# Two attention layers with experts on one core: projections moved among the first scores and beside the routing, score tiles issued around the transposed pair

## What is computed

```
x = x + tanh(g_xattn[0]) * attention0(layernorm(x), ctx)     # 16 heads of 16
x = x + tanh(g_ffn[0])   * experts(layernorm(x))             # 8 experts, top 2, weights 256x256
x = x + tanh(g_xattn[1]) * attention1(layernorm(x), ctx)
x = x + tanh(g_ffn[1])   * bitlinear_ffn(layernorm(x))       # 256 -> 1024 -> gelu -> 256, activations to 8 bit, weights ternary

attention: q = x Wq^T + bq, k = ctx Wk^T + bk, v = ctx Wv^T + bv
           softmax(q k^T / 4) v, heads joined, times Wo^T, plus bo
```

## Time and profile before

| | us |
|---|---|
| time, median of 3 runs (lowest, highest) | 765.19 (763.31, 765.99) |
| the profiled execution, its time | 762.36 |
| the profiled execution, its span | 760.5 |
| PE busy | 690.9 (91%) |
| DVE busy | 534.3 (70%) |
| ACT busy | 432.4 (57%) |
| POOL busy | 164.2 (22%) |
| mean granted TensorE clock | 0.973 |

### The profile page before, as it was taken

The page is one execution under the profiler, slowest core; times in us unless marked ns, Lnnn a source line. Parts: engine busy times, 40 slices in busy tenths (PEclk is TensorE's granted clock), DMA queues, the critical chain, the costliest instruction groups (busy, mean ns, idle before and its releaser), DMA issues.

```text
span 760.5 us, 10162 instructions
## 1 busy us (share of the span) xinstructions
PE 690.9 (91%) x3595; PEld 331.7 (44%) x3600; DVE 534.3 (70%) x1140; ACT 432.4 (57%) x568; POOL 164.2 (22%) x300
## 2 busy tenths in 40 slices
PE   4899999899999999998999989998999899987887
PEld 2433333354544445444554445443444344332444
DVE  2577886578886687868787688865686749775334
ACT  2227666763346633665336733476776677758735
POOL 7105244630010310121101410114210301021132
PEclk9769999999999999999999999999999999999999
DMA  7749578521211501224211411126023212200000
GB/s 242 205 126 335 181 226 266 169 55 32 42 43 29 167 11 34 61 80 98 44 36 37 125 44 43 43 71 199 11 64 91 77 50 57 58 2 1 22 8 28
DMA packets 39026, 66.74 MB, mean 88 GB/s; under 512 B 5184, under 2 KB 13888, under 8 KB 38720
## 3 DMA queue, kind: packets, MB, share of 16 engines
q1 hardware_dynamic: 38128, 65.57, 30.0%
q10 hardware_dynamic: 848, 0.53, 0.2%
HBM read 38.29 MB, written 27.26 MB: 86 GB/s over the span
## 4 chain that ended last, share of the span: by engine, by line
PE 59%; DVE 14%; ACT 10%; issue 8%; POOL 8%; POOLq 0%; DVEq 0%; ACTq 0%
PE psO L799 11%; PE psS L771 8%; PE psX L724 6%; PE psT L785 6%; DVE mx L1194 6%; PE psX L860 5%; PE psX L836 4%; PE psX L861 4%; PE psX L862 4%; ACT pt L1017 3%; PE psX L744 3%; POOL parts L588 2%; DVE xs L1325 2%; ACT qf L962 2%; ACT parts L963 1%
## 5 line engine op out<-in xcount | busy, mean ns | idle before, releaser
L1017 ACT ACTIVATE pt<-psT 128x1024 f32<-128x1024 f32 x256 | 261.7, 1022 | 220.6 <-PE psT L785 218.1
L1194 DVE TENSOR_REDUCE mx<-psS 128x1 f32<-128x512 f32 x512 | 325.7, 681 | 80.5 <-PE psS L771 79.1
L771 PE MATMUL psS<-ks,qs 48*128 48x512 f32 x512 | 152.5, 514 | 15.2 <-DVE mx L1194 13.8
L799 PE MATMUL psO<-pt,vg 128*32 128x512 f32 x1024 | 139.5, 618 | 0.1
L785 PE MATMUL psT<-qs,ks 50*128 50x512 f32 x512 | 118.8, 428 | 6.9 <-ACT pt L1017 5.8
L771 PEld LDWEIGHTS psS<-ks,qs 48*128 48x128 f32 x512 | 59.9, 189 | 130.0 <-issue 73.1
L1325 DVE SCALAR_TENSOR_TENSOR xs<-psX,coef,xs 128x256 f32<-128x256 f32 x128 | 61.9, 483 | 32.4 <-PE psX L862 29.2
L588 POOL TENSOR_TENSOR parts<-qf,parts 128x512 fp32r<-128x512 f32 x30 | 38.3, 1278 | 147.2 <-ACT parts L963 147.2
L785 PEld LDWEIGHTS psT<-qs,ks 50*128 50x128 f32 x512 | 52.6, 189 | 22.4 <-ACT pt L1017 19.5
L860 PE MATMUL psX<-moeh,xh 128*128 128x512 f32 x128 | 57.4, 449 | 4.4 <-DVE xs L1325 4.4
L861 PE MATMUL psX<-moel,xh 128*128 128x512 f32 x128 | 50.7, 396 | 0.0
(11 more groups left out here) (129 smaller groups left out, 765.3 us busy)
## 6 DMA issues: line engine op xcount, KB each, us to landing
ks<-kd SPq DMA_DIRECT2D x64, 192.0 KB, 3.5
qs<-qd SPq DMA_DIRECT2D x64, 192.0 KB, 4.3
kd<-parts SPq DMA_DIRECT2D x16, 512.0 KB, 3.2
qd<-parts SPq DMA_DIRECT2D x16, 512.0 KB, 2.7
kd<-parts SPq DMA_DIRECT2D x16, 256.0 KB, 4.1
qd<-parts SPq DMA_DIRECT2D x16, 256.0 KB, 3.4
ctxb<-in_ctxT SPq DMA_DIRECT2D x7, 512.0 KB, 4.7
xs<-in_x SPq DMA_DIRECT2D x4, 512.0 KB, 6.1
```

The costliest lines, as they stand in the source:

```text
L771: mm(psS[:, i % 3, :], qs[at:at + KR, 2 * g + a, k * P:(k + 1) * P], ks[at:at + KR, 2 * g + a, :], start=True, stop=True).then_inc(pe_s, 1)
L799: i = mm(psO[32 * j:32 * j + 32, :], vg[:, p % 2, k, g * GH + j, :], pt[:, s % RING, j, :], start=k == 0, stop=k == NT - 1, tile_position= ...
L1017: a(pt[:, G % RING, 2 * half:2 * half + 2, :], psT[:], ACT.Exp, scale=SCALE).then_inc(a_exp, 1)
L1194: v.tensor_reduce(mx[:, w // GH % 2, r, col:col + 1], psS[:, i % 3, :], AX.X, ALU.max).then_inc(v_max, 1)
```

## The change

1. Slot order: S of (w, half) is issued as two separate items; one score tile (upper rows), then both transposed tiles with the lower rows first, then the other score tile (lower rows), then PV and the slot's pieces. `s_pair` becomes `s_tile`, and the maxima on DVE follow one by one.
2. The four SPLITs of stage 1 (K and Q) leave slots 0, 2, 4 and 6 of stage 0. K 0 goes ahead of the lead, K 1 to slot -10, Q 0 to slot -7, Q 1 to slot -4; the second XT of sequence 1 moves to slot -12.
3. The two K SPLITs of stage 3 move from slots 0 and 2 of stage 1 to slots 16 and 18.
4. In stages 1 to 4 the VV pieces move from slots 11 and 15 to 6 and 10. In stages 2 to 4 the second layer norm, its XT and its two Q SPLITs move from slots 3 to 10 to slots 13 to 18, beside the routing. (The layer norm's two coefficient sets are then used in swapped order: the `swap` argument.)
5. In stages 5 to 7 both XB stand at slot 15 instead of one at 14 and one at 15.
6. XQ and HQ have four small DVE steps instead of five, and POOL waits for three of them.
7. For the very first and the very last layer norm the small steps run on DVE (LNE, LND), with only the power on POOL; in the tail they stand in another order, and BUSY shrinks from 29 + 4 + 4 + 9 to 20 + 4 + 4.

```diff
     lead = -1
+    put(lead, 20, ("XT", (1,)))
     put(lead, 21, ("RELOAD", (0, 2)))
-    put(lead, 22, ("RELOAD", (0, 3)))
+    put(lead, 22, ("RELOAD", (0, 3)), ("SPLIT", ("K", 1, 1)))
+    put(lead, 25, ("SPLIT", ("Q", 1, 0)))
+    put(lead, 28, ("SPLIT", ("Q", 1, 1)))
...
-    put(0, 0, ("SPLIT", ("Q", 1, 0)), ("LD", ("x3",)))
+    put(0, 0, ("LD", ("x3",)))
     put(0, 1, ("LD", ("w1",)))
-    put(0, 2, ("SPLIT", ("K", 1, 0)))
     put(0, 3, ("LNC", (2, 0, NT)), ("LD", ("w2",)))
-    put(0, 4, ("SPLIT", ("Q", 1, 1)), ("LD", ("k1",)))
-    put(0, 5, ("LNN", (2, 0, 2)))
-    put(0, 6, ("SPLIT", ("K", 1, 1)), ("LNN", (2, 2, 4)))
+    put(0, 4, ("LD", ("k1",)))
+    put(0, 5, ("LNN", (0, 2, 0, 2)))
+    put(0, 6, ("LNN", (0, 2, 2, 4)))
...
-    pair(1, 0, "SPLIT", "K", 3, step=2)
+    pair(1, 16, "SPLIT", "K", 3, step=2)
...
-                put(p, 11, ("VV", (p + 1, 0)))
-                put(p, 15, ("VV", (p + 1, 1)))
+                put(p, 6, ("VV", (p + 1, 0)))
+                put(p, 10, ("VV", (p + 1, 1)))
...
+        two = 2 <= p <= B
         if 2 <= p <= B + 1:
             st(p, 1, p - 2, NT - 1)
             put(p, 1, ("LNC", (p - 2, 0, NT)))
-            put(p, 3, ("LNN", (p - 2, 0, 2)))
-            put(p, 4, ("LNN", (p - 2, 2, 4)))
+            put(p, 20, ("BIAS", (p - 2, 1)))
+        if p == B + 1:
+            put(p, 3, ("LNN", (0, p - 2, 0, 2)))
+            put(p, 4, ("LNN", (0, p - 2, 2, 4)))
             pair(p, 5, "XT")
             pair(p, 9, "SPLIT", "Q", B + p - 2)
-            put(p, 20, ("BIAS", (p - 2, 1)))
...
+            if two:
+                put(p, 13, ("LNN", (1, p - 2, 0, 2)))
+                put(p, 14, ("LNN", (1, p - 2, 2, 4)))
+                pair(p, 15, "XT", step=0)
+                pair(p, 16, "SPLIT", "Q", B + p - 2, step=2)
...
-            put(p, 14, ("XB", (0, 1, 0, NT)))
-            put(p, 15, ("XB", (1, 2, 0, NT)))
+            put(p, 15, ("XB", (0, 1, 0, NT)), ("XB", (1, 2, 0, NT)))
...
-    put(NP, 4, ("OP", (1, b, 0)), ("ST", (b, 0)), ("ST", (b, 1)), ("LNC", (b, 0, 2)), ("LNN", (b, 0, 2)))
-    put(NP, 4, ("OP", (1, b, 1)), ("ST", (b, 2)), ("ST", (b, 3)), ("LNC", (b, 2, 4)))
-    put(NP, 4, ("BUSY", (29,)))
-    put(NP, 5, ("XQ", (0, 2)), ("LNN", (b, 2, 4)), ("XB", (0, NC, 0, 2)), ("BUSY", (4,)), ("XQ", (2, 4)))
-    put(NP, 5, ("F1", (0,)), ("XB", (0, NC, 2, 4)), ("BUSY", (4,)), ("F1", (1,)), ("F1", (2,)), ("F1", (3,)),
-        ("BUSY", (9,)))
+    put(NP, 4, ("OP", (1, b, 0)), ("ST", (b, 0)), ("ST", (b, 1)), ("LNE", (b, 0, 2)), ("OP", (1, b, 1)))
+    put(NP, 4, ("LND", (b, 0, 2)), ("LNN", (0, b, 0, 2)), ("ST", (b, 2)), ("ST", (b, 3)))
+    put(NP, 4, ("LNE", (b, 2, 4)), ("LND", (b, 2, 4)))
+    put(NP, 4, ("BUSY", (20,)))
+    put(NP, 5, ("XQ", (0, 2)), ("LNN", (0, b, 2, 4)), ("XB", (0, NC, 0, 2)), ("BUSY", (4,)), ("F1", (0,)))
+    put(NP, 5, ("XQ", (2, 4)), ("XB", (0, NC, 2, 4)), ("BUSY", (4,)), ("F1", (1,)), ("F1", (2,)), ("F1", (3,)))
...
-    out = [("ST", (0, t)) for t in range(NT)] + [("LNC", (0, 0, NT)), ("SPLIT", ("K", 0, 0)), ("LNV", ())]
+    out = [("ST", (0, t)) for t in range(NT)] + [("LNE", (0, 0, NT)), ("LND", (0, 0, NT)), ("SPLIT", ("K", 0, 0)), ("LNV", ())]
...
-    out += [("VV", (0, 0)), ("VV", (0, 1)), ("LNN", (1, 0, NT))] + [("XT", (c,)) for c in range(NC)]
+    out += [("VV", (0, 0)), ("VV", (0, 1)), ("LNN", (0, 1, 0, NT))]
+    out += [("SPLIT", ("K", 1, 0)), ("XT", (0,))]
...
         if 0 <= w < NP * H:
-            out.append(("S", (w, half)))
+            out.append(("S", (w, half, 0)))
         if 0 <= G < NP * H:
             out.append(("T", (G, half)))
+        if 0 <= w < NP * H:
+            out.append(("S", (w, half, 1)))
...
-                for r in range(2):
+                for r in (1, 0):
                     at = HALF * r
                     i = mm(psT[:, r, :], ks[at:at + KR + MP, 2 * g + half, k * P:(k + 1) * P],
...
+            def variances(b, t0, t1):
+                ...
+                v.tensor_scalar(lnw[:, i, 5, t0:t1], mv[:, i, t0:t1, 1], LN_EPS, None, ALU.add).then_inc(v_ln, 1)
...
+            def coefficients(b, t0, t1):
+                ...
+                v.tensor_tensor(t, r0, r0, ALU.mult).then_inc(v_ln, 1)
...
+                v.tensor_tensor(t, t, ve, ALU.mult).then_inc(v_ln, 1)
...
+                v.tensor_scalar(t, t, -0.5, 1.5, ALU.mult, ALU.add).then_inc(v_ln, 1)
...
+                v.tensor_tensor(r1, r0, t, ALU.mult).then_inc(v_ln, 1)
...
+                v.scalar_tensor_tensor(out=nb, in0=mean, scalar=-1.0, in1=r1, op0=ALU.mult, op1=ALU.mult
+                                       ).then_inc(v_ln, 1)
...
-                v.tensor_scalar(big, big, Q_EPS, None, ALU.max).then_inc(v_hq, 1)
+                v.tensor_scalar(big, big, Q_EPS, 1.0 / 127.0, ALU.max, ALU.mult).then_inc(v_hq, 1)
                 if due(v_hq, i + 2):
                     dve.wait_ge(v_hq, i + 2)
+                v.reciprocal(inv, big).then_inc(v_hq, 1)
                 v.tensor_scalar(deq, big, dqf[:, 1:2], None, ALU.mult).then_inc(v_hq, 1)
-                v.reciprocal(inv, big).then_inc(v_hq, 1)
-                if due(v_hq, i + 4):
-                    dve.wait_ge(v_hq, i + 4)
-                v.tensor_scalar(inv, inv, 127.0, None, ALU.mult).then_inc(v_hq, 1)
```

131 lines of the change are left out of this document (81 added, 50 removed).

## The result

The changed kernel takes 775.47 us (median of 4 executions, 774.1 to 782.5) against 765.53 (763.31 to 765.99); the ratio is 1.0171, 95% interval [1.0138, 1.0205]. Forecast were 745 and faster. The profiled execution took 776.58, its span is 774.8 against 760.5.

A forecast was written before the change was run, and what follows sets the result against it. PE was taken as the bound, with time won only where it waits or runs at 1.2 GHz. Terms 0 - 7.5 - 3 - 4.5 - 3.5 + 0 - 1.5 = -20 us took 765.2 to 745, range 734 to 758.

The forecast's parts named there:

- Start and lead: Up to the first exponential: earlier first S (-2.5 us) offsets the projections and XT added to the lead (+2.8); sum 0.
- so I take the other two at full clock, 0.5 us each with the turn: Lead: only the first of three SPLITs meets the low clock; the other two starve DVE 0.5 us each.
- the sign of success: First exponential at 46 to 50 us would show the forecast right.
- Stage 0: Slots 0 to 8 without their four SPLITs take 17 us instead of 24.5, a gain of 7.5.
- Rival 3: Clock: lead stays at 1.2 GHz, stage 0's slots 0 to 2 and the tail's F1 slow; 753 us, chance 0.10.
- Stage 1: Moving two K SPLITs to slots 16 and 18, and a VV to slot 6, gains 3 us.
- won from the clock: Stage 1: about 1.5 us gained because the clock, at 0.98 there, would be fuller.
- Stages 2 to 4: Moved XT and SPLITs fill the 1.43 us routing wait; -1.5 us a stage, -4.5 in all.
- XB, XQ, HQ: Stages 5 to 7: XB at slot 15 fills PE's wait for POOL, with fewer steps; -1, -2 and -0.5 us.
- The slot order: T freed from a waiting second S gains 8 us; lone second S tiles behind T cost 8; sum 0.
- Tail: Behind the last exponential: nine fewer BUSY matmuls save 1.94 us, first XQ begins about 1.3 later; -1.5 us.
- rival 4: Slower: second S behind a waiting T becomes the rule, lone tiles costing up to 34 us; 779 us, chance 0.11.

The follow-up runs named there:

- e5: Kernel before with only the first layer norm's steps on DVE, shorter XQ and HQ, and both XB in slot 15; 757.9 us.
- e2: Changed kernel with the four projections for the second batch back in slots 0, 2, 4 and 6 of stage 0; 774.9 us.
- e10: e5 with the four projections of stage 0's slots 0 to 6 moved into the lead; 765.3 us.
- e7: Changed kernel with eight unread filler matmuls added at the end of each of the lead's twelve half steps; median 778.3 us, profiled execution 767.4.
- e17: e5 with stage 1's two K projections moved from slots 0 and 2 to slots 16 and 18; 761.6 us.
- e9: e5 with the change's moves of projections and layer norm in stages 1 to 4 on top; 759.9 us.
- e3: Changed kernel with the projections and layer norm of stages 1 to 4 back where they stood before; 773.3 us.
- e12: e5 with the first XB back in slot 14; 763.5 us.
- e6: e5 with the new order of score tiles on top; 765.3 us.
- e4: Changed kernel with the old tail: old filler, layer norm on POOL, second XQ ahead of the first F1; 775.4 us.
- e8: Changed kernel with only the second half's XQ put ahead of the first F1 again, shorter filler kept; 774.5 us.
- e11: e5 with the tail in the changed order and 20, 4 and 4 BUSY matmuls; 766.1 us.
- e1: Changed kernel with both score tiles ahead of the transposed tiles again, as in the kernel before; 770.0 us.
- e15: e5 with the first value projection in slot 6 instead of 11, in each of four stages; 779.7 us.
- e13: e9 with the second value projection in slot 11 instead of 10; 759.4 us.

## Why the prediction was wrong

Two steps carry most of the miss. The prediction took the granted clock, outside the places that it edited, as it had been before (terms of 0), and the change put 35 us more at 1.2 GHz, some 10.8 us of time. And without the clock the -20 don't come either: by the "at 50" column e5's parts give -4.3 us, the order +4.2, the lead with stage 0 +1.2, the tail +2.0, the moves of stages 1 to 4 -3.7, and all together +2.0, where the forecasts were -6 (with the first S), 0, -4.7, -1.5 and -7.5. These are estimates, with an error of about 1 us for a part and 4 for all together. Part by part:

**Start and lead (forecast 0, bounds -3 to +6).** Without the SPLITs the start is 4.0 us earlier (e5), not 2.5. But the projections and XT in the lead cost 6.9 us (e2 against the changed kernel) to 11.0 (e10), not 2.8. The step that failed is "so I take the other two at full clock, 0.5 us each with the turn": it was the first that met the full clock (DVE idle 1.13 us where I had 2.4), and the other two ran at 1.2 GHz and cost DVE 2.83 and 3.44 us. The 0.5 is too small even at full clock: there e7 has 1.58 and 2.42. DVE bounds the lead, so nearly all of this idle time, 7.4 us, goes into the start. The fourth SPLIT, ahead of the lead, I priced at nothing; the first S comes 0.3 to 0.7 us later with it (28.04 us against 27.77 in e2 and 27.39 in e5). The first exponential, at 50.8 us, stands outside the 46 to 50 that I gave as the sign of success.

**Stage 0 (forecast -7.5, bounds -9.5 to -4).** It came to -1.3, and -2.6 in e10. I priced the four SPLITs at their places and took the clock behind the lead as full, because it had been so. With 19 us of it at 1.2 GHz, slots 0 to 8 take 22.8 us where I wrote 17; in e7's profiled execution, with 6.8 us at 1.2 GHz, they take 19.1. Rival 3 named this mechanism (+1.5 for slots 0 to 2) and sized it far too small: it lasted to 70 us.

**Stage 1 (forecast -3).** The K move alone is -1.2 in its own stage (e17) and +2.7 to +3.7 in all, though this loss is hardly clear of the scatter. The routing's wait of 1.42 us was filled as forecast. But the 1.5 us "won from the clock" didn't come: stage 1 of e17 has 3.4 us at 1.2 GHz (0.98), as before. The step that failed is that a stage's gain can be booked alone.

**Stages 2 to 4 (forecast -4.5, bounds -8 to 0).** PE's idle time fell from 3.8 to 2.9 us a stage, and at equal clock all the moves together give -3.7. The thinner cover of the layer norm's chain costs PE two waits of 0.6 us in slots 11 and 12, and the wait of 1.43 us at the routing is gone. What I put at nothing was the clock: +6.3 over the three stages in the profiled execution. The moves bring 15 and 18 us more at 1.2 GHz (e9 against e5, the changed kernel against e3). The upper bound of 0 was wrong: nothing in the rows excluded a loss.

**XB, XQ, HQ (forecast -3.5).** Right in the sum, and by luck in its parts. XB gives -3.0 at equal clock and -5.5 in the medians (e12 against e5). In stage 6 the reason held: the stage is 4.4 us shorter and its clock full. But in e5 stages 5 and 7, from which I had -1 and -0.5, are 0.0 and +1.3.

**The slot order (forecast 0, bounds -8 to +12).** It costs 7.3 us (e6), 4.2 at equal clock. That S and T overlap was right: the slots with ME keep 2.25 and 3.25 us. The lone tile of 0.22 us fits the sign and the stages, and +8 stood as a bound. What failed is the -8 against it: a T freed from a waiting S meets an exponential that isn't done. The 11.5 us won at S came back as 10.6 at T. ACT would then be the second late one in those slots, which the earlier trace rows gave a hint of (T's 46 waits), and I counted 35 slots as if it weren't. This reading rests on the totals; the slots weren't followed one by one.

**Tail (forecast -1.5, bounds -3 to +2).** It is +5.9, of which 4.8 is DVE's wait for the first Gelu (e4, e8), and e11 gives 4.6 for it; the other 1.1 is the stricter wait of POOL in e5 and e4, which I had not read at all. I followed XQ(0, 2) past the moved layer norm, and didn't follow XQ(2, 4) past F1(0). The diff showed the swap of two items, and the wait stands in `xq()` of both kernels. It showed in no view of before, since no F1 stood ahead of XQ(2, 4) there; asking which waits the moved instruction brings along would have found it. The shorter filler, which rival 3 feared, costs nothing that the tail's length shows (39.0 us in e8 as in e4).

**The whole.** The time lies outside the range, 734 to 758, beside rival 4 (779, chance 0.11). Its mechanism, the second S behind a waiting T, is real, but it costs 5.5 to 7.3 us (e1, e6) of the 34 that it was sized at; the rest of the loss came from the clock and from the tail's wait, so rival 4 came near the time by luck. Rival 3 had its mechanism and gave it 0.10 and 753 us. It asked where the clock would fall at the edited places, and took the rest as it was. Measured, the change puts 35 us more at 1.2 GHz, at 0.31 us each 10.8 of the 12.8 us between the means. The parts don't add up: each of the four large parts on top of e5 adds 12 to 17 us at half clock, all together 40 and not 60, and their differences in the medians (7.3, 7.4, 8.1 and 2.0) would give 782.7 where 775.5 was measured. That the low clock causes the longer time, and doesn't merely go with it, is shown by stage 2 of e17, the same instructions with less idle time and 3.7 us more. Why the clock falls stays open. One projection moved lowers it (e15), by the hole or by the fuller slot. Less idle time doesn't keep it (e13), and it falls behind work behind which it stays full in e5 (e17).

## What to carry to other kernels

Where PE is busy over 90% and the clock is nearly full, the clock is a resource that an edit can lose in stages that it doesn't touch; give every move in such a kernel a clock term with an upper bound, and judge it by several executions with the granted clock beside each. A projection can be worth more among other work than its own length: moved by five slots, it cost 21.8 us. When an order is changed between two loops, subtract from the gain of the one what the other is late by. For every instruction moved past another, ask which waits it brings along, and whether a wait by count asks for more than the data need.

## What the runs showed of the hardware

The mean granted clock of one program differs between its executions (e10: 0.953 to 0.975, 103 executions of before: 0.962 to 0.975), and with it the time: 758.5 to 768.8 us in e10, and in e9 two groups 4.5 us apart with nothing between. The Trainium skill (TensorE: Matmul & The Clock Gate, What's actually happening) says that the monitor behind the clock runs free of the kernel's start. The scatter of e9 and e7 would fit that and doesn't show it. A us at 1.2 GHz costs 0.31 us here by the regression; stage 2 of e17 shows why it is under a half: with 10.2 us at 1.2 GHz PE is busy 4.6 us longer, and idle 0.9 less, since some of its waits are filled.

The clock can fall with PE busy nearly throughout. In e17 PE is idle 0.11 us in the 7.2 us before the clock falls at 254.2:

```profile
247.00:250.60 3.60, 3.60 (x25) 1.65 (x23) 2.78 (x5) 3.60 (x8) 0.95 (x3) 1.00 0.55 218
250.60:254.20 3.60, 3.49 (x28) 2.56 (x24) 1.69 (x3) 3.02 (x5) 1.22 (x1) 1.00 0.63 158
```

The Trainium skill (TensorE: Matmul & The Clock Gate, What's actually happening) also says that the throttled state is the default and activity releases it. More activity went with a fuller clock in the lead: 0.52 from the first S to the first exponential in e5, 0.82 with three SPLITs and an XT more (the changed kernel), 1.00 with filler (e7's profiled execution). The fall in e17 it doesn't explain: PE was as busy there as in e5, whose clock stayed.
